# Two chunks of unit rows shared with DVE, and the fourth scores ahead of the seventh group's transposes, in a two-layer graph kernel

## The reference

```python
# x [4096,128] f32, adj [4096,4096] of 0 and 1 (diagonal 1), beta [1], weight [128,128]
norm2  = jnp.linalg.norm(x, axis=1, keepdims=True)
cos    = beta[0] * (x @ x.T) / (norm2 @ norm2.T + 1e-07)
masked = cos + (1.0 - adj) * -1000000000.0
x1 = _layernorm(x + jax.nn.softmax(masked, axis=1) @ x)
out = _layernorm(x1 + adj @ (x1 @ weight))
```

## Time and profile before

| | |
|---|---|
| median of 3 runs | 484.43 us (483.68 to 484.55) |
| the profiled execution | 484.12 us, its span 482.3 us |
| mean granted PE clock | 0.993 |
| PE busy | 470.6 us (98%) |
| DVE busy | 382.3 us (79%) |
| ACT busy | 319.6 us (66%) |
| POOL busy | 59.7 us (12%) |

### The profile page before, as it was taken

The page is one execution under the profiler, slowest core; times in us unless marked ns, Lnnn a source line. Parts: engine busy times, 40 slices in busy tenths (PEclk is TensorE's granted clock), DMA queues, the critical chain, the costliest instruction groups (busy, mean ns, idle before and its releaser), DMA issues.

```text
span 482.3 us, 8977 instructions
## 1 busy us (share of the span) xinstructions
PE 470.6 (98%) x3551; PEld 309.2 (64%) x3551; DVE 382.3 (79%) x600; ACT 319.6 (66%) x375; POOL 59.7 (12%) x75
## 2 busy tenths in 40 slices
PE   8799999999999999999999999999999999999995
PEld 7456667667676666767666676766764444444484
DVE  4889999999999999999999999999974043222363
ACT  5988988898898889889888988988862000000000
POOL 5811010110210020120102002000100000000011
PEclk9899999999999999999999999999999999999998
DMA  8999999999999999989996997960052000111102
GB/s 199 92 137 103 121 103 119 101 116 141 122 133 126 129 119 119 143 115 94 153 126 79 130 125 121 83 135 22 0 175 67 22 23 22 45 43 45 43 24 65
DMA packets 101530, 46.78 MB, mean 97 GB/s; under 512 B 69376, under 2 KB 98944, under 8 KB 101504
## 3 DMA queue, kind: packets, MB, share of 16 engines
q0 software_dynamic: 20064, 16.78, 42.6%
q1 hardware_dynamic: 81152, 29.63, 31.3%
q10 hardware_dynamic: 288, 0.07, 0.1%
HBM read 73.99 MB, written 22.81 MB: 201 GB/s over the span
## 4 chain that ended last, share of the span: by engine, by line
PE 89%; POOL 3%; DMA 3%; DVE 1%; issue 1%; ACT 1%; SPq 0%; POOLq 0%; DVEq 0%
PE psum L1002 23%; PE psum L1062 20%; PE psum L1006 12%; PE psum L979 11%; PE psum L980 11%; PE psum L981 11%; POOL rn L390 2%; POOL adjT L396 1%; DMA adjT<-in_x 1%; DMA uT<-x_parts 1%; DMA E<-x_rows 1%; DMA out<-E 0%; PE psum L1078 0%; POOL adj_bytes L386 0%; POOL rstd L415 0%
## 5 line engine op out<-in xcount | busy, mean ns | idle before, releaser
L1002 PE MATMUL psum<-xaug,eh 128*128 128x257 f16 x1024 | 184.7, 274 | 0.4 <-DVE uT L595 0.3
L473 ACT ACTIVATE E<-psum,sc 128x1024 f32<-128x1024 f32 x128 | 154.3, 1205 | 36.5 <-PE psum L981 35.5
L1006 PE MATMUL psum<-xaug,el 128*128 128x129 f16 x1024 | 175.8, 221 | 0.0
L715 DVE SCALAR_TENSOR_TENSOR E<-E,adjT 128x1024 f32<-128x1024 f32 x128 | 156.4, 1222 | 10.0 <-ACT E L473 9.1
L723 DVE SCALAR_TENSOR_TENSOR el<-E,eh 128x1024 f16<-128x1024 f32 x128 | 156.2, 1220 | 0.0
L482 ACT ACTIVATE eh<-E 128x1024 f16<-128x1024 f32 x128 | 134.4, 1050 | 3.0 <-DVE E L715 2.6
L1002 PEld LDWEIGHTS psum<-xaug,eh 128*128 128x128 f16 x1024 | 99.3, 98 | 26.4 <-DVE el L723 1.3
L1062 PE MATMUL psum<-adjT,uT 128*128 128x512 fp8e4 (+1 forms) x576 | 112.3, 356 | 0.5 <-DMA uT<-x_parts 0.5
L1006 PEld LDWEIGHTS psum<-xaug,el 128*128 128x128 f16 x1024 | 100.4, 98 | 14.2
L979 PE MATMUL psum<-uT 128*128 (+1 forms) x256 | 97.8, 382 | 0.4 <-ACT E L473 0.4
L980 PE MATMUL psum<-uT 128*128 (+1 forms) x256 | 97.6, 381 | 0.0
(11 more groups left out here) (83 smaller groups left out, 189.3 us busy)
## 6 DMA issues: line engine op xcount, KB each, us to landing
adj_bytes<-in_adj POOLq DMA_DIRECT2D x27, 512.0 KB, 11.4
adj_bytes<-in_adj POOLq DMA_DIRECT2D x9, 256.0 KB, 6.2
x_rows<-x SPq DMA_DIRECT2D x8, 256.0 KB, 2.9
E<-x_rows SPq DMA_DIRECT2D x8, 256.0 KB, 3.0
out<-E SPq DMA_DIRECT2D x16, 128.0 KB, 2.2
x_parts<-x1p SPq DMA_DIRECT2D x7, 256.0 KB, 4.0
adjT<-in_x SPq DMA_DIRECT2D x3, 512.0 KB, 6.7
uT<-x_parts SPq DMA_DIRECT2D x2, 512.0 KB, 5.6
```

Of the source, the lines that this page charges most:

```text
L473: nc.scalar.activation(E[:, m % RING, :, :], S[m % 2], ACT.Exp, bias=col(C_BB), scale=col(C_BS)).then_inc(e_done, 1)
L715: nc.vector.scalar_tensor_tensor(out=e, in0=e, scalar=EPRE, in1=mask_bytes(b, m), op0=ALU.mult, op1=ALU.min).then_inc(masked, 1)
L1002: return nc.tensor.matmul(O[t][:, 0:XC], eh[:, s, a, cols], xaug[:, j, :], start=start, stop=stop)
L1006: return nc.tensor.matmul(O[t][:, 0:D + 1], el[:, s, a, cols], xaug[:, j, 0:D + 1], start=False, stop=False)
```

## The change

Chunk 1: ACT makes the first six tiles, DVE the last two, right behind low part 0. Chunk 3: POOL makes the first four tiles, DVE the last four, behind low part 1 and ahead of the load of the flag. `unit_rows` gets a first tile for this, `wait_unit_rows` now goes by groups, and the counts of `u_done` move by one or two. On PE, groups 6 and 7 are both turned after the fourth scores (m = 3); group 6 stood before them. The same arithmetic is done on the same values.

```diff
--- before.py
+++ after.py
@@ -253,14 +253,17 @@
         def chunk(c):
             return slice(c * CT, (c + 1) * CT)
 
-        def wait_unit_rows(engine, c):
-
-            if c == 1:
+        def wait_unit_rows(engine, g):
+
+
+            if g in (2, 3):
                 engine.wait_ge(u_done_a, 1)
-            elif c == NC - 1:
+                if g == 3:
+                    engine.wait_ge(u_done, 2)
+            elif g == UG - 2:
                 engine.wait_ge(u_done_p, 1)
             else:
-                engine.wait_ge(u_done, (1, None, 2)[c])
+                engine.wait_ge(u_done, {0: 1, 1: 1, 4: 3, 5: 3, 7: 4}[g])
 
         def uT_out(part, g):
             return uT[:, part, g * 512:(g + 1) * 512].rearrange("q (c p a) -> q c a p", c=2, a=2)
@@ -392,7 +395,7 @@
 
             def unit_rows_p(c):
                 pool.wait_ge(rn_done, c + 1)
-                for t in range(c * CT, (c + 1) * CT):
+                for t in range(c * CT, c * CT + CT // 2):
                     last = nc.gpsimd.tensor_scalar(work[:, t, :], xfull[:, t, :], rn[:, t:t + 1], USC, ALU.mult, ALU.mult)
                 last.then_inc(u_done_p, 1)
 
@@ -451,7 +454,7 @@
                 act.wait_ge(rn_done, c + 1)
                 nc.scalar.activation(rn_a[:, :], rn[:, chunk(c)], ACT.Copy, scale=USC).then_inc(rn_scaled, 1)
                 act.wait_ge(rn_scaled, 1)
-                for t in range(CT):
+                for t in range(CT - 2):
                     last = nc.scalar.activation(work[:, c * CT + t, :], xfull[:, c * CT + t, :], ACT.Copy,
                                                 scale=rn_a[:, t:t + 1])
                 last.then_inc(u_done_a, 1)
@@ -584,10 +587,11 @@
                 dve.wait_ge(squares_a, c + 1)
                 nc.vector.tensor_scalar_max(n2[:, chunk(c)], n2[:, chunk(c)], 1e-36).then_inc(n2_done, 1)
 
-            def unit_rows(c):
+            def unit_rows(c, first=0):
                 dve.wait_ge(rn_done, c + 1)
-                nc.vector.scalar_tensor_tensor(out=work[:, chunk(c), :], in0=xfull[:, chunk(c), :], scalar=USC,
-                                               in1=rn[:, chunk(c)].unsqueeze(2).to_broadcast([P, CT, D]),
+                ts = slice(c * CT + first, (c + 1) * CT)
+                nc.vector.scalar_tensor_tensor(out=work[:, ts, :], in0=xfull[:, ts, :], scalar=USC,
+                                               in1=rn[:, ts].unsqueeze(2).to_broadcast([P, CT - first, D]),
                                                op0=ALU.mult, op1=ALU.mult).then_inc(u_done, 1)
 
             def uT_lo_part(g):
@@ -640,6 +644,7 @@
             clamp(3)
             partition_extremes()
             uT_lo_part(0)
+            unit_rows(1, CT - 2)
             tiny_norms()
             unit_rows(2)
             scale_step(1)
@@ -647,6 +652,7 @@
             scale_step(3)
             scale_step(4)
             uT_lo_part(1)
+            unit_rows(NC - 1, CT // 2)
             small = dve.value_load(flag[0:1, 0:1], min_val=0, max_val=1)
 
             def invert_norms():
@@ -944,7 +950,7 @@
             pe.wait_ge(consts, 4)
 
             def turn_unit_rows(g):
-                wait_unit_rows(pe, g * 4 // CT)
+                wait_unit_rows(pe, g)
                 if g > 3:
                     pe.wait_ge(uT_lo, g - 4 + 1)
                 for t in range(4):
@@ -1037,8 +1043,8 @@
                     turn_unit_rows(4)
                 if m == 2:
                     turn_unit_rows(5)
+                if m == 3:
                     turn_unit_rows(6)
-                if m == 3:
                     turn_unit_rows(7)
                 if m == LAG0:
```

## The result

The changed kernel took **487.77 us** (median of 8 runs, 482.47 to 489.17) and the kernel before, on the same chip in the same minutes, 484.06 (8 runs, 483.01 to 485.47): ratio **1.0058, 95% interval 1.003 to 1.0087**. (The ratio is not the quotient of the two medians, which is 1.0077.) It is slower where 0.2% faster was forecast, and the median lies outside the range of 482.4 to 484.7. Sorted, its runs read 482.47, 483.6, 485.82, 487.57, 487.98, 488.52, 488.98, 489.17. A median of so scattered a set is not the size of one effect, so the first thing to find out is what differs between its quick and its other executions. (Run again beside other kernels the changed kernel came to 485.11 and 484.73, each of 12 runs.

The account below looks back on a forecast made before the run. DVE was taken to bound the stretch from 17 to 52 us, PE the rest. -1.27 + 0.1 + 0.1 - 0.1 = -1.2 us gave 482.9 against the profiled execution, plus 0.31 for the median: 483.2, range 482.4 to 484.7.

Parts of the forecast that it names:

- DMAs: Fifth cast moves from 21.69 to about 18.5; third transposition keeps 0.7 us slack before pair 2's mask, taken as enough.
- Rival 3: Third transposition lands behind the earlier cast, at 29.0; pair 2's mask 1.9 us later, 486.3 us; chance 0.06.
- POOL: Chunk 3, four rows fewer: rows end by 18.5 instead of 21.73, cost nothing, hidden by the fourth scores.
- PE's order: Fourth scores from 19.4 to 20.7, group 7 at about 22.3; gap before uT_lo part 7 goes whole, -1.27 us.
- DVE: Two added instructions: 128x256 behind uT_lo part 0 taken as 0; 128x512 behind part 1 +0.1, and +0.1 for POOL's rows.
- rival 1: DVE's load and branch wait for the new 128x512: +0.65 in place of +0.1, 483.8 us; chance 0.25.
- The up to +0.36 on DVE: At DVE's 128x512: by the skill's rule, a POOL row in flight could cost up to +0.36 instead of +0.1.
- ACT: Chunk 1, two tiles fewer, 0.6 us: first exponential 0.3 to 0.4 sooner than 15.50, worth nothing.
- Rival 2: Clock falls in PE's new gap, lower level at 26 for 3.4 us: gain 0.25, 484.2 us; chance 0.10.
- 0.50 anywhere after 25: Sign that the forecast as a whole is wrong: granted clock at 0.50 anywhere after 25 us.
- Rival 4: All of PE's loss comes back, 2.38 idle and about 1.1 for slow matmuls: 481.0 us; chance 0.03.
- Rival 5: Nothing: before's median already holds part of the gain, 484.4 us; chance 0.11 together with a transposition eating part.

Follow-up runs that it names:

- a_third: The changed kernel unedited, run once more: 484.73 us, ratio 1.0005; its profiled execution took 489.83.
- a_free_both: Changed kernel, pairs 2 and 3 of block 0 and 8 to 11 of block 1 masked with other pairs' bytes, waits moved later (timing only): 484.16 us.
- w_twice: Changed kernel with the fifth scores computed twice, filling PE's gap before the first weighing: 484.23 us, ratio 1.0007.
- a_free2: Changed kernel, pairs 2 and 3 of block 0 masked with other pairs' bytes, third transposition waited for at pair 4 (timing only): 483.36 us.
- a_again: The changed kernel again, nothing edited: 485.11 us, ratio 1.0005.
- b_early: Kernel before with the fifth cast alone moved up between POOL's fourth and fifth row of chunk 3: 484.88 us, ratio 1.0034.
- b_split: Kernel before, POOL waiting for the second transposition between its fourth and fifth row, fifth cast after all eight rows: 484.26 us, ratio 1.0021.
- a_late3: Changed kernel with SP holding the third transposition back until DVE's low part 3 is done: 486.18 us, ratio 1.0028.
- order_only: Kernel before with PE's order alone changed, all eight rows still on POOL: 483.17 us, ratio 0.9985.
- hold_b: Changed kernel with POOL's fifth and later casts held until DVE's low part 3 is done, second run of it: 483.82 us, ratio 0.9996.
- a_free_b1: Changed kernel, block 1 and pairs 2 and 3 of block 0 masked with block 0 bytes already there, no block 1 mask waited for (timing only): 483.27 us.

## Why the prediction was wrong

**The step that failed** is the one under *DMAs*: "After the change that mask wants it at 25.85: 0.7 us of slack, taken as enough. Later masks have 3 us and more." Both sentences are wrong. The prediction's own sign of it, a wait of DVE for a DMA before the mask of pair 2, is there in a_third (2.28 us). The slack at pair 2 was 0.37 us in the quick profile of the change (1.24 in a_free_both, 2.53 in w_twice), and in the other sort of execution the landing is 2.6 us and more behind that quick one's: I knew one draw. "3 us and more" was true of block 0's later pieces in before (3.9 at least), but not after the change (2.7 at pair 4 and 2.4 at pair 6), and block 1's third piece had 1.98 us in before (landed 82.66, wanted at 84.64), of which the gain takes 1.5 unless the piece lands sooner too (in the quick profile it did, at 81.06). Before's DVE row, without a wait:

```profile
84.64 1.21 DVE L715 SCALAR_TENSOR_TENSOR E<-E,adjT 128x1024 f32<-128x1024 f32 x1
```

And lateness is not absorbed between these places but handed on from cast to transposition to cast.

**Rival 3** had this mechanism ("If the transposition's data go behind that cast"), with a landing of 29.0; measured were 27.8 to 30.1. It was wrong in two sizes. Its chance was set at 0.06 from one trace in which the transposition landed in time; five of the nine profiles with the early cast show it late. And its price was pair 2's wait alone (486.3, deciding from 28.1); in a_third and a_free2 the larger waits are in block 1, and PE's slower clock behind them comes on top, so the change's upper runs reach 491.5. What spoke against it, that the longest transposition took 8.6 us, was a maximum of a kernel in which this cast did not go out in this place: with the early cast the late ones take 9.5 to 12.2 (18.67 to 28.17, 17.99 to 30.14).

**The other steps held.** *POOL*: rows ended at 18.36 (predicted by 18.5). *PE's order*: 19.26, 20.55 and 22.24 for scores, group 6 and group 7 (19.4, 20.7, 22.3); the gap went whole. *DVE*: the 128x256 cost nothing; for the 128x512 +0.2 was booked and -0.1 measured, so the load and the branch ran beside it altogether and rival 1 is out. The Trainium skill (Advanced Engine Details and Errata, "Sequencer Loop") says that other instructions can be queued while control work executes: the trace agrees, 17.07 to 17.70 without idle. Of POOL's rows the one that began just behind DVE's 128x512 took 0.91 in place of 0.36, and DVE's piece took 0.71, against 0.67 in a_again, where it began at 18.27, beside POOL's last row:

```profile
17.10 0.91 POOL L399 TENSOR_SCALAR adjT<-adjT,rn 128x128 f32<-128x128 f32 x1
```

The up to +0.36 on DVE did not come; POOL's row in flight ended at 17.11, 0.04 after DVE's start, so no run puts it to the test. The Trainium skill (SBUF — State Buffer, "Who interferes with whom"), from which I had it, says of DVE's two-port modes that whoever issues first has the shared pair for the whole instruction, and of two SBUF inputs only that they contend; POOL's 0.91 agrees, and no run shows it for DVE. *ACT*: worth nothing as said, but for another reason: the "0.3 to 0.4 sooner" of its first exponential did not come, because the flag and not the scores holds it. *Rival 2*: not in the gap ahead of the first weighing; no profile of the changed rows or order has the lower clock between 25 and 35. Its sign, "0.50 anywhere after 25", did come, but behind a wait for a mask (a_third from 92.0, a_free2 from 91.5), as a part of rival 3's price. *Rival 4*: out. *Rival 5*: in part. Of the 70 runs of before in the first two sets, 37 with a mean clock of 0.996 or more have a median of 483.31 and the other 33 one of 484.03, so before's own median probably holds executions that never lost the clock at 21.5 (a run without a profile tells only its mean clock); lowest against lowest, the change gains 0.4 us (482.19 and 482.58), not 1.2. Even without its upper runs it would hardly have been measurable: the 14 runs of the change up to 485 have a median of 483.7, those of before 483.5.

**What is shown and what stays open.** Shown: a late third transposition was seen only with the early cast, and those profiles are the slower ones; the lateness reaches block 1 and block 2 with or without DVE's wait at pair 2, though not always (b_early); holding the cast back in the changed kernel thins the upper runs out. Argued, not shown: that each unprofiled upper run is of this sort, that the early cast alone makes the loss (b_early and its control are not apart), that a late transposition alone does (a_late3 and before are not apart in their set), and why half of b_early's shift is there without the cast (b_split). Open: what decides in a given execution whether transposition and cast land together, in which order block 1's pieces are then served, and what the upper runs of order_only and of before are made of, of which no profile was taken. That the change is slower in the median is also not equally firm in all sets: 1.0058 once, 1.0005 twice.

## What to carry to other kernels

When a change speeds up the consumer of a stream and moves a DMA of that stream forward, read the slack of every transfer of the chain in the profile, not of the first, and find out by the waits between its producers whether a late link delays all the following ones. One profiled execution gives one draw of a DMA's landing; a slack of 0.4 to 2.5 us against a landing that varies by 7 (22.7 to 30.1 in the nine profiles with the early cast) is a chance and not a cover. And when two parts of a change reach the same gap, try each alone first: here the order alone (483.17), or the shared rows alone with the cast held back (483.13), closed the gap that both closed, with the cast near its old time.

## What the runs showed of the hardware

- A transposing DMA issued near 18 and a 256 KB cast issued 0.6 to 0.8 us behind it end either apart (25.20 and 27.02) or together to within 0.15 us (27.77 and 27.78; 28.60 and 28.60; 30.14 and 30.01), the transposition then taking 9.5 to 12.2 us in place of 4.6 to 6.8. With the cast issued at 21.7 or later it took 4.2 (hold_b) to 7.4 (b_split) in eight profiles.
- A queue of casts and transpositions that wait for each other can carry a lateness of 5 us at 30 us on to 107 us (a_free_b1): block 2's first piece landed at 107.76 where DVE wanted it at 104.9; in the quick profile of the change it landed at 101.07.
- A 128x512 DVE instruction (0.71) placed ahead of a load of a register and a branch cost nothing where the gap of the load and branch had been 0.65.
- After PE had stood 2.64 us, its granted clock was at the lower level (0.50, 1.2 GHz) from 92.0 to 95.0 (a_third), so a wait for a DMA cost more than its own length.
- ACT's first exponential behind a load of a flag started 1.10 to 1.11 us after DVE began the flag, in all 20 profiles.
